# Writing out the five main loops of a graph attention kernel

## The reference

```python
Eh = (edge_attr @ WE).reshape(-1, H, D)
score = jnp.einsum('ehd,ehd,ehd->eh', Kh[src], Qh[dst], Eh) * inv_sqrt_d
score = jnp.exp(jnp.clip(score, -5.0, 5.0))
msg = Vh[src] * score[:, :, None]
wV = jax.ops.segment_sum(msg, dst, num_segments=N)
Z = jax.ops.segment_sum(score, dst, num_segments=N)
h_out = wV / (Z[:, :, None] + 1e-06)
x = _layernorm(x + h_out.reshape(N, H * D), axis=-1)
```

## Time and profile before

| | |
|---|---|
| median of 3 runs | 3138.6 us (3130.92 to 3141.23) |
| span of the profiled execution (the time that its page gives) | 3220.4 us |
| instructions in it | 56767 |
| TensorE busy | 2141.5 us (66%) |
| VectorE busy | 1538.8 us (48%) |
| ScalarE busy | 1316.4 us (41%) |
| GpSimd busy | 1547.9 us (48%) |
| mean granted clock of TensorE | 0.758 |

### The profile page before, as it was taken

One profiled execution on the slowest core, in us unless ns is written; L12 is line 12 of the kernel. 1 busy time (PEld: TensorE's weight loads), 2 busy tenths in 40 slices (PEclk: granted clock), 3 DMA queues, 4 the chain that ended last, 5 costly groups with the idle time before them and its releaser, 6 DMA issues.

```text
span 3220.4 us, 56767 instructions
## 1 busy us (share of the span) xinstructions
PE 2141.5 (66%) x14786; PEld 1940.1 (60%) x14787; DVE 1538.8 (48%) x3801; ACT 1316.4 (41%) x3270; POOL 1547.9 (48%) x1628
## 2 busy tenths in 40 slices
PE   6566666666766666666766666666666666666666
PEld 5466656665655666665666556656556665666565
DVE  4444444454444544444444444444444444544446
ACT  2344443444434444344444344443444444444343
POOL 3444444454544445444545444544444554445542
PEclk8677777777777777777777777777777778777777
DMA  7533333333333333333333333333333333333331
GB/s 214 150 102 100 105 102 103 103 101 101 107 102 102 102 103 105 102 101 103 101 106 103 103 102 99 104 104 102 103 102 100 106 105 101 102 104 105 104 105 56
DMA packets 222816, 339.98 MB, mean 106 GB/s; under 512 B 92112, under 2 KB 117688, under 8 KB 222795
## 3 DMA queue, kind: packets, MB, share of 16 engines
q0 software_dynamic: 77376, 211.39, 22.2%
q1 hardware_dynamic: 144843, 128.08, 14.7%
q10 hardware_dynamic: 576, 0.26, 0.0%
HBM read 325.24 MB, written 9.60 MB: 104 GB/s over the span
## 4 chain that ended last, share of the span: by engine, by line
another core or an unknown queue 32%; PE 22%; issue 21%; DVE 15%; DVEq 7%; ACT 2%; ACTq 1%; DMA 0%; SPq 0%
PE psW L578 12%; PE psE L544 4%; DVE msg L919 4%; DVEq L244 4%; PE psT L535 3%; DVE acc L936 3%; PE psH L554 2%; DVE prod L897 2%; DVE prod L902 2%; DVE score L907 1%; DVEq L936 1%; DVEq L948 1%; ACT hot L709 1%; DVEq L894 1%
## 5 line engine op out<-in xcount | busy, mean ns | idle before, releaser
L434 POOL DMA_INDIRECT kv<-kv_table,src_idx x1612 | 1539.4, 955 | 1620.1 <-DVE msg L919 1118.6
L578 PE MATMUL psW<-msg,hot 128*128 128x136 f32 x3224 | 665.3, 367 | 462.3 <-DVE msg L919 461.5
L722 ACT ACTIVATE attrT<-psT 128x512 f32<-128x512 f32 x403 | 240.8, 597 | 1665.2 <-remote 1213.7
L578 PEld LDWEIGHTS psW<-msg,hot 128*128 128x128 f32 x3224 | 567.3, 257 | 522.3 <-DVE msg L919 380.4
L544 PE MATMUL psE<-w_e,attrT 128*128 128x128 f32 x3224 | 592.2, 320 | 177.6 <-issue 175.6
L902 DVE TENSOR_TENSOR prod<-prod,psQ 128x512 f32<-128x512 f32 x403 | 276.8, 687 | 855.4 <-remote 848.5
L567 PE MATMUL psQ<-Qp,hotT 128*128 x4836 | 458.3, 242 | 265.4 <-issue 263.9
L544 PEld LDWEIGHTS psE<-w_e,attrT 128*128 128x128 f32 x3224 | 517.8, 234 | 193.0 <-issue 191.7
L567 PEld LDWEIGHTS psQ<-Qp,hotT 128*128 128x128 bf16 x4836 | 365.3, 110 | 371.0 <-issue 364.2
L709 ACT ACTIVATE hot<-iota,local 128x128 f32 x1612 | 512.0, 390 | 4.4 <-issue 2.5
L897 DVE TENSOR_TENSOR prod<-kv,psE 128x512 f32<-128x512 f32 x403 | 277.2, 688 | 339.9 <-issue 170.8
(11 more groups left out here) (94 smaller groups left out, 362.5 us busy)
## 6 DMA issues: line engine op xcount, KB each, us to landing
attr<-in_edge_attr_dram SPq DMA_DIRECT2D x403, 256.0 KB
kv<-kv_table,src_idx POOLq DMA_INDIRECT x1612
src_idx<-in_src_dram SPq DMA_DIRECT2D x403, 2.0 KB
kv_table<-kv SPq DMA_DIRECT2D x12, 512.0 KB, 3.8
Qp<-Qp SPq DMA_DIRECT2D x23, 192.0 KB
hot<-in_x_dram SPq DMA_DIRECT2D x12, 256.0 KB, 4.4
xT<-in_x_dram SPq DMA_DIRECT2D x8, 384.0 KB
out_dram<-xT SPq DMA_DIRECT2D x46, 64.0 KB
```

What stands on the lines that cost most here:

```text
L434: nc.gpsimd.indirect_dma_start(out=kv[:, u, t, :], out_offset=None, in_=kv_table, in_offset=bass.IndirectOffsetOnAxis(ap=src_idx[:, u, t:t ...
L578: last = nc.tensor.matmul(psW[:, u % 2, 0:MW], hot[:, u % HOTS, t, :], msg[:, u % 2, t, :], start=(t == 0), stop=(t == TILES - 1))
```

## The change

The five loops over turns become Python loops, so that each turn's instructions are written out and each threshold and each address that depends on the turn alone is a constant. The table loads at the head of each turn stay, and so do the addresses that come from them.

```diff
@@ -348,10 +348,10 @@
-            with sp.Fori(2, LAG + 2) as b:
+            for b in range(2, LAG + 2):
                 load_turn(b)
 
-            with sp.Fori(LAG + 2, B_LAST) as b:
+            for b in range(LAG + 2, B_LAST):
                 load_turn(b)
                 store_window(b - (LAG + 2))
@@ -439,7 +439,7 @@
-            with pool.Fori(1, B_LAST) as b:
+            for b in range(1, B_LAST):
                 for u in range(RINGS):
                     gather(b, u)
@@ -608,7 +608,7 @@
-            with pe.Fori(1, B_LAST) as b:
+            for b in range(1, B_LAST):
                 slots = load_slots(b * RINGS + 1, RINGS)
                 for u in range(RINGS):
                     step(b, u, slots[u])
@@ -761,7 +761,7 @@
-            with act.Fori(1, B_LAST) as b:
+            for b in range(1, B_LAST):
                 odd = load_odd(b * RINGS + 3, RINGS)
                 for u in range(RINGS):
                     step(b, u, odd[u])
@@ -1001,12 +1001,12 @@
-            with dve.Fori(1, LAG) as b:
+            for b in range(1, LAG):
                 windows = load_windows(b * RINGS - 1, RINGS)
                 for u in range(RINGS):
                     step(b, u, windows[u])
             dve.wait_ge(x_res_in, 16 * (RINGS + 1))
-            with dve.Fori(LAG, B_LAST) as b:
+            for b in range(LAG, B_LAST):
                 windows = load_windows(b * RINGS - 1, RINGS)
                 for u in range(RINGS):
                     step(b, u, windows[u], b - LAG)
```

## The result

The changed kernel takes 3034.4 us (median of 4, 3030.34 to 3043.2) beside 3139.9 us (median of 4, 3130.92 to 3145.64) of the kernel before: ratio 0.9667, 95% interval [0.9643, 0.9691]. The profiled spans are 179 us apart (3220.4 and 3041.3); the one of before lies 75 us above even the slowest of its timed runs, so periods read from the two traces overstate the gain. No profile of the kernel before at 3139 us exists.

A forecast was written before the change was run, and what follows sets the result against it. The prediction took a chain of hand-overs, with news late while gathers run, to bound the kernel. Loop ends -6, threshold arithmetic 0 and code reading +3 gave -3 us: 3138.6 to 3135 us, rounded down, range 3070 to 3175.

The forecast's parts named there:

- What bounds the kernel: Main loops: a chain of hand-overs between engines, no engine's throughput, with news late while gathers run; 15.46 us per two groups.
- the period and its four parts: Two groups on VectorE, 15.46 us: 5.42 between `msg` products, 1.48 to the gather, 6.23 to L902, 2.33 to next `msg`.
- All of this is engine time: Said of the 5.42 us between a pair's two `msg` products: TensorE sums and turns, ScalarE copies and runs `exp`.
- Threshold arithmetic, 0 us: Queue operations for waits counted in groups: removing them gains 0 us, at most 51 us, as queues run ahead of engines.
- the 6.23 us stretch: From the second group's first gather to VectorE's L902, which waits for TensorE's finished `psQ` until the pair's gathers are through.
- My own last sentence: Sign of being wrong altogether: the 6.2 us stretch shrinks or grows everywhere, so the instruction count moves what closes the way.
- Rival A: Fewer TensorE queue operations let `q_sel` news through before gathers close the way: 54 us less, 3085 us; chance 0.26 with C.
- Loop ends, -6 us: Branch and counter at each of 49 turn ends: removing them saves 0.12 us a turn, bounds -17 and 0.
- within 0.3 us of the others: Sign of being right: the period across a turn's end differs from the other periods by no more than this.
- Reading the code, +3 us: Instruction fetches of written-out code, about 3 packets a turn on a DMA engine, cost 0.06 us a turn; bounds 0 and +146.
- Rival B: Code reading goes on the path, on TensorE in the 5.42 us or VectorE or ScalarE during gathers: 3184 us; chance 0.21.
- Rival C: Threshold arithmetic is on the path after all, 0.13 us in each step, 51 us less; counted with A, together 0.26.

## Why the prediction was wrong

- *What bounds the kernel.* Right for the 3135 us level in that late news bounds it: the period and its four parts stand, 5.42 and 1.48 are unchanged after, and halving the gathers took the late news away. "All of this is engine time" left out that TensorE works through the 5.42 us at the lower clock (0.50), which it gets to in the wait.
- *Threshold arithmetic, 0 us.* This step failed, and with it the reading that the 6.23 us stretch "depends on the gathers" and so not on the change. I argued that queue operations count only where a queue is itself late, because queues run ahead of their engines. At this level, writing out the loops of the four engines other than TensorE, which sends the late news, moved it: L902 came 3.2 us behind the gather instead of 6.2 in three periods of four, and the kernel took 3032.1 us instead of 3139.1. Which queue operations do it, and by what way, stays open. VectorE's L897, let go 1.1 to 1.8 us late before and at once after, points at what VectorE waits for or does ahead of the gather; no run of VectorE's loops alone met this level. Queue operations were themselves held in the kernel before: 428 of 17396 took 0.6 to 0.8 us (DMA issues and table loads not counted). In the changed kernel it is 52 of 10648, with TensorE's loop kept 89 of 11384, and none in the profiles of the variants at 2139 us. That they and the news wait for the same thing is argued from these counts, not shown.
- *My own last sentence* ("if the 6.2 us stretch shrinks ... the way is closed by something that the instruction count moves") is what happened. The argument against it came from the prologue, where ScalarE's wait lasts until the last gather: that shows that a long run of gathers closes the way with few instructions about, but not that fewer instructions can't get news through before a short run of eight.
- *Rival A.* The mechanism that it names at VectorE (L902 early, 1.1 us a period) came true, in three periods of four and not in one: 3 x 1.0 x 49 is the 152 us above, where I had 54. Its cause was misplaced: I put it on TensorE's queue, and TensorE's loop gives nothing beyond the others'. That the timed gain is 105 us and not 152 and more says again that the trace before overstates.
- *Loop ends, -6 us.* Undersized, and "within 0.3 us of the others" was wrong: the period across the turn's end is now 1.0 us longer than the others (10.01 against 9.0), as the table reads stay there and the news is late in 39 of 44. Reading the excess under a cover of 3.12 us was the error; its own gain was 24 us at most, by the traces.
- *Reading the code, +3 us.* 4.9 packets more a turn and not 3: I had read TensorE's queue alone, and the same view of the first turn has 3 packets of q14 beside it. There is no cost that any run could tell from none: with TensorE's loop kept, which saves 123 of the packets, the ratio is the same 0.967. Rival B is refuted.
- *Rival C.* With half of the gathers the loop ends and the arithmetic are worth 49 us, near its price of 51, but by luck: in the middle steps nothing went (3.78 us in both), so it is above all the turn's end and not each step.

Open: which of the four engines' queue operations matter, VectorE's own or others', or whether it is their number; what makes the kernel take 3135 or 2139 us; and what the 0.3 to 0.6% is that TensorE's written-out loop costs at 2139 us.

## What to carry to other kernels

A wait that ends for "remote", long after the awaited work is done and just as another engine's run of work ends, is a bound that queue operations can move, also those of engines that do not send the news; put a real chance on any change of queue work there, however little engine work it touches. Look then at all that the waiting engine does ahead of the wait, and not only at the wait itself. Price an edit's small item where nothing covers it: the loop end read 0.35 us under a 3 us wait and 0.55 to 0.9 us without it. And take the baseline beside each variant: here it moved by a third between sessions, and the same change gave 0.967 at one level and 1.003 at the other.

## What the runs showed of the hardware

- The same kernel takes 3124 to 3146 us in some sessions and 2136 to 2145 us in others, on one chip too. At the 3135 us level news between engines and some queue operations are late while indirect gathers run; at 2139 us neither is, with gathers running nearly without a pause.
- At the 3135 us level TensorE's granted clock is 0.50 (1.2 GHz) behind the wait of nearly every period (174 of 176), and the eight sum matmuls there take 2.18 us instead of 1.15 at 1.00.
- At the 2139 us level the gathers are the bound, 1.25 us each (0.95 and 0.30 between two), 128 rows of 1 KB a gather.
- Writing out 49 turns on five engines reads 3.2 MB of code in 260 packets beside 340 MB of data, at no cost that could be measured.
